# Block attention: the weighing step moved to another place of the round, with 32 named output columns and two buffers of weights

## What is computed

```python
q, k, v = heads(h @ Wq.T), heads(h @ Wk.T), heads(h @ Wv.T)
scores = einsum('bhsd,bhjkd->bhsjk', q, kb) * SCALE
scores = where(diag_mask, -inf, scores)
w = softmax(scores, axis=-1)
w = w * include
out = einsum('bhsjk,bhjkd->bhsd', w, vb)
norm = sum(w, axis=(-2, -1))
o = out / (norm + 1e-06)
return merged(o) @ Wo.T
```

## Time and profile before

| | us |
|---|---|
| median of three runs | 6166.44 |
| the profiled execution | 6168.93 |
| its span | 6167.2 |
| TensorE busy (matmul) | 5278.3 (86%) |
| VectorE busy | 3368.0 (55%) |
| ACT busy | 2937.9 (48%) |
| GpSimd busy | 1177.3 (19%) |

### The profile page before, as it was taken

One profiled execution on the slowest core, in us unless ns is written; L12 is line 12 of the kernel. 1 busy time (PEld: TensorE's weight loads), 2 busy tenths in 40 slices (PEclk: granted clock), 3 DMA queues, 4 the chain that ended last, 5 costly groups with the idle time before them and its releaser, 6 DMA issues. The chain is left out here.

```text
span 6167.2 us, 90780 instructions
## 1 busy us (share of the span) xinstructions
PE 5278.3 (86%) x31918; PEld 3935.3 (64%) x31918; DVE 3368.0 (55%) x6363; ACT 2937.9 (48%) x8715; POOL 1177.3 (19%) x1352
## 2 busy tenths in 40 slices
PE   4799998999989999899997899798879596399968
PEld 2677877877778877778776556455545354255545
DVE  3576676666667666676665333355551654443231
ACT  1566666666666666666664111144441243315421
POOL 1222222222222222223222000111100321002210
PEclk6899999999999999999998999799999798588879
DMA  1000000000000000000001000100000100000000
GB/s 39 15 18 18 16 18 17 18 18 16 15 17 22 18 14 16 18 18 22 13 16 47 1 1 1 70 1 1 0 17 10 23 1 10 28 1 1 1 21 14
DMA packets 49430, 97.37 MB, mean 16 GB/s; under 512 B 12704, under 2 KB 20032, under 8 KB 47840
## 3 DMA queue, kind: packets, MB, share of 16 engines
q1 hardware_dynamic: 48992, 91.77, 5.1%
HBM read 87.28 MB, written 2.38 MB: 15 GB/s over the span
## 5 line engine op out<-in xcount | busy, mean ns | idle before, releaser
L857 ACT ACTIVATE dh_pb<-bank 64x128 f32<-64x128 f32 x3072 | 829.1, 270 | 273.5 <-PE bank L631 239.9
L645 PE MATMUL bank<-dh_cw,dh_pb 128*128 128x128 f32 x5120 | 701.6, 281 | 112.6 <-ACT dh_pb L857 111.1
L645 PEld LDWEIGHTS bank<-dh_cw,dh_pb 128*128 128x128 f32 x5120 | 635.9, 193 | 190.6 <-ACT dh_pb L857 163.9
L995 DVE SCALAR_TENSOR_TENSOR dh_kq<-bank,dh_conv_kq,dh_kq 128x511 f32<-128x511 f32 (+2 forms) x408 | 305.5, 749 | 185.1 <-ACT dh_kq L814 173.9
L863 ACT ACTIVATE dh_cw<-bank 128x256 f32<-128x256 f32 x640 | 244.5, 384 | 255.4 <-PE bank L645 248.1
L582 PE MATMUL bank<-hT,dh_w_kq 128*128 128x512 f32 x544 | 277.7, 635 | 82.7 <-DVE dh_kq L995 75.4
L995 DVE SCALAR_TENSOR_TENSOR dh_v<-bank,dh_conv_v,dh_v 128x511 f32<-128x511 f32 (+2 forms) x384 | 284.2, 747 | 91.2 <-ACT dh_v L814 82.2
L1669 PE MATMUL bank<-moe_h_split,moe_w 128*128 x1200 | 279.7, 383 | 22.2 <-PEq L88 14.9
L594 PE MATMUL bank<-dh_w_vz,hT 128*128 128x256 f32 x1024 | 245.5, 383 | 22.0 <-ACT dh_zs L825 22.0
L582 PE MATMUL bank<-hT,dh_w_vz 128*128 128x512 f32 x512 | 242.5, 596 | 8.5 <-DVE dh_v L995 8.5
L1508 ACT ACTIVATE moe_mlp_silu<-bank 128x512 f32<-128x512 f32 x100 | 59.7, 597 | 394.3 <-PE bank L1675 394.3
(11 more groups left out here) (412 smaller groups left out, 12263.1 us busy)
## 6 DMA issues: line engine op xcount, KB each, us to landing
dh_rates<-delta_rates SPq DMA_DIRECT2D x130, 256.0 KB, 3.6
dh_w_vz<-in_L_wvz SPq DMA_DIRECT2D x17, 512.0 KB, 3.4
mod_w<-in_L_wmod SPq DMA_DIRECT2D x4, 1536.0 KB, 6.8
dh_w_kq<-in_L_wkq SPq DMA_DIRECT2D x18, 256.0 KB, 2.6
dh_wo<-in_L_wo SPq DMA_DIRECT2D x16, 256.0 KB, 4.2
moe_w<-in_L_w13T SPq DMA_DIRECT2D x1, 3200.0 KB, 16.1
x_res<-in_x SPq DMA_DIRECT2D x1, 2048.0 KB, 8.4
mla_wA<-in_L_wA SPq DMA_DIRECT2D x1, 2048.0 KB, 8.0
```

The source lines that it names most:

```text
L645: last = pe.matmul(square(j)[:, b, :, :], pb[j][:, b, :], src[:, :, b, :], start=True, stop=True)
L857: last = act.activation(out[half, :, o, half], src[halves[o], :, half], ACT.Copy)
L995: dve.scalar_tensor_tensor(y, pj_bank(n)[:, 0:S - i], taps(n)[:, TAPS - 1 - i:TAPS - i], y, ALU.mult, ALU.add).then_inc(s["v_cs" if i < TA ...
```

## The change

It moves `weigh` and `shape` on TensorE and VectorE, gives `weights` two buffers, lets `weigh` name 32 output columns for each head (its own 16 features and the 16 that follow in `values`, so the rows of bank 7 between heads hold the next head's result), pads `values` by one head of zeros, puts `oT` into `k.hT`, which is free by then, and makes `tmp` one buffer.

```diff
-        wt = ph.sb("weights", [P, HPG, NC * (NC + 1) // 2 * P])
+        wt = ph.sb("weights", [P, 2 * HPG, NC * (NC + 1) // 2 * P])
...
-        oT = ph.sb("oT", [P, 2, HPG, S])
-        tmp = ph.sb("tmp", [P, 2, 2, D])
+        oT = k.hT
+        tmp = ph.sb("tmp", [P, 2, D])
...
-                            last = pe.matmul(bank[7][32 * i:32 * i + DK2, j * P:S], values[:, b, j, g * HPG + i, :],
-                                             wt[:, i, TURNED_AT[j]:TURNED_AT[j] + (NC - j) * P], start=(j == 0),
+                            head = (b * NC + j) * H2 + g * HPG + i
+                            two = values[:, head:head + 2, :].rearrange("p h n -> p (h n)")
+                            last = pe.matmul(bank[7][32 * i:32 * (i + 1), j * P:S], two,
+                                             wt[:, G % 2 * HPG + i, TURNED_AT[j]:TURNED_AT[j] + (NC - j) * P], start=(j == 0),
                                              stop=(j == NC - 1), skip_group_check=True)
...
-                pe.wait_ge(zero, 1)
+                pe.wait_ge(zero, 2)
...
                     if first: first_pass(G - 1, 0)
-                    if doing["weigh"](G): weigh(G - LAG - 1)
                     if second: second_pass(G - LAG, 0)
...
                     if first: first_pass(G - 1, 2 * RING)
                     if second: second_pass(G - LAG, 2 * RING)
+                    if doing["weigh"](G): weigh(G - LAG - 1)
                     if first: first_pass(G - 1, 3 * RING)
                     if second: second_pass(G - LAG, 3 * RING)
...
-                        after(dve, added, n - 1)
-                        dve.tensor_tensor(tmp[:, i, :, :], ring(("out", b, i))[:, :].rearrange("p (t d) -> p t d", t=2),
+                        after(dve, added, n)
+                        dve.tensor_tensor(tmp[:, :, :], ring(("out", b, i))[:, :].rearrange("p (t d) -> p t d", t=2),
...
                 dve.memset(mx[:, :, :, :], 0.0).then_inc(zero, 1)
-                dve.wait_ge(zero, 1)
+                dve.memset(values[:, NB * NC * H2:, :], 0.0).then_inc(zero, 1)
+                dve.wait_ge(zero, 2)
...
                     if doing["score"](G): maximum(G, 0)
-                    if doing["weigh"](G): shape(G - LAG - 1)
                     if doing["score"](G): maximum(G, 1)
                     if doing["score"](G): maximum(G, 2)
+                    if doing["weigh"](G): shape(G - LAG - 1)
...
-                    after(act, summed if first else weighed, G)
-                    act.activation((e if first else wt)[:, i, at:at + width], ring((which, G, n))[:, 0:width], ACT.Exp)\
+                    after(act, summed if first else weighed, G if first else G - 1)
+                    out = e[:, i] if first else wt[:, G % 2 * HPG + i]
+                    act.activation(out[:, at:at + width], ring((which, G, n))[:, 0:width], ACT.Exp)\
...
-        values = ph.sb("values", [P, NB, NC, H2, DK2])
+        values = ph.sb("values", [P, NB * NC * H2 + 1, DK2])
```

More of the change, by code:

```diff
@@ L2664, in _ @@
                         act.wait_ge(vproj, 2 * b + i + 1)
-                        act.activation(values[:, b, 2 * i:2 * i + 2, :, :].rearrange("p t h n -> p (t h n)"), bank[i][:, :],
-                                       ACT.Copy).then_inc(vkept, 1)
+                        act.activation(values[:, (b * NC + 2 * i) * H2:(b * NC + 2 * i + 2) * H2, :].rearrange("p h n -> p (h n)"),
+                                       bank[i][:, :], ACT.Copy).then_inc(vkept, 1)
         ph.clear()
@@ L2867, in add_out @@
                         xs = k.x[:, b, 2 * i:2 * i + 2, :]
-                        dve.tensor_tensor(xs, xs, tmp[:, i, :, :], ALU.add).then_inc(added, 1)
+                        dve.tensor_tensor(xs, xs, tmp[:, :, :], ALU.add).then_inc(added, 1)
                 dve.memset(mx[:, :, :, :], 0.0).then_inc(zero, 1)
-                dve.wait_ge(zero, 1)
+                dve.memset(values[:, NB * NC * H2:, :], 0.0).then_inc(zero, 1)
+                dve.wait_ge(zero, 2)
                 for G in rounds:
@@ L2914, in clear_corners @@
                         pool.wait_ge(upto, nth(G, HPG * n + i))
-                        ev = t[:, i, at:at + (1024 if n == 1 else 2 * P)].rearrange("p (a n) -> p a n", a=2)[:, :, 0:P]
+                        ev = t(G)[:, i, at:at + (1024 if n == 1 else 2 * P)].rearrange("p (a n) -> p a n", a=2)[:, :, 0:P]
                         pool.affine_select(ev, ev, [[0, 2], [1, P]], ALU.is_ge, 0.0, channel_multiplier=-1).then_inc(done, 1)
                 for G in rounds:
[L2919 to L2922, removed]
+                    if doing["first"](G): clear_corners(lambda G: e, masked1, expd1, G - 1, 0, 1)
+                    if doing["second"](G): clear_corners(lambda G: wt[:, G % 2 * HPG:G % 2 * HPG + HPG], masked2, expd2, G - LAG, 0, 1)
+                    if doing["first"](G): clear_corners(lambda G: e, masked1, expd1, G - 1, 896, 2)
+                    if doing["second"](G): clear_corners(lambda G: wt[:, G % 2 * HPG:G % 2 * HPG + HPG], masked2, expd2, G - LAG, 896, 2)
         ph.clear()
```

## The result

The changed kernel takes **6181.03 us** (median of 20 runs, 6175.69 to 6195.77), the kernel before 6166.07 us in the same session (20 runs, 6159.76 to 6173.71): a ratio of 1.0024, interval 1.0017 to 1.0030. It is slower by 15 us, where 6148 us, 18 us less than before, were forecast. The profiled execution took 6180.93 us (span 6179.2); that of before took 6168.93 (span 6167.2).

The account below looks back on a forecast made before the run. TensorE, busy 86% of the span, was taken as the bound. Steady part -11.5 us, table load +1.8 and tail -8.4 gave -18.1 from the median of 6166.44: 6148 us, range 6140 to 6158.

Parts of the forecast that it names:

- the place: Steady round at full clock: moving the weighing late costs 0.67 us a round, +6.0 us over nine rounds.
- table load: Rounds 10 and 14: the early weighing also hid ACT's table load of 0.90 us; moving it costs +1.8 us.
- the tail: Rounds 16 to 22: gains and losses by round sum to -8.4 us, ends -13 and -4.
- clock term: Steady part: half clock costs 2.95 us a round, of which a third, 1.0 us, stays; -17.5 us.
- the stretch of 71%: Third triples of both passes in round 12: TensorE busy only 71%, right before the clock fell.
- the 87% of F1, S1 and C: Second triples of both passes and the scores after them, round 12: TensorE busy 87%, not followed by a fall.
- rival 3: The weighing runs at half clock, 4.45 us for 2.28: 6176 or 6190 us; decides from 3.0 us a round; chance 0.10.
- Rival 2: Steady part: the clock falls as often as now, each round costs 0.67 us more: 6166 us; chance 0.23.
- F0 to S0: First second-pass triple to first third-pass triple: 1.90 us once the weighing leaves, -1.45 us a round.
- S0 to F1: First third-pass triple to second second-pass triple, scores between: +0.41 us a round, waiting for banks.
- S2 to W: Third third-pass triple to the weighing now behind it: 1.3 us, where 1.87 led to the next triple, -0.57.
- F3 with S3: Fourth triples of both passes: 2.3 us at full clock, between a floor of 2.0 and a ceiling of 3.51.

Follow-up runs that it names:

- run 9: Kernel before, with extra matmuls behind the second and third second-pass triples and the third third-pass triple, none behind the fourth second-pass triple: 6143.53 us, ratio 0.9960.
- run 4: Changed kernel with four extra matmuls of 384 columns behind each of the first three second-pass triples in rounds 7 to 15: 6152.19 us, ratio 0.9979.
- run 7: Changed kernel with the extra matmuls of run 4 behind the second and third second-pass triples only: 6153.52 us, ratio 0.9983.
- run 8: Changed kernel with the extra matmuls of run 4 behind the first second-pass triple only: 6179.12 us, ratio 1.0021.
- run 3: Changed kernel with the weighing split in three parts, one behind each of the first three second-pass triples: 6166.88 us, ratio 0.9996.
- run 1: Changed kernel with the weighing and its shaping back at the old place, columns and buffers kept: 6167.77 us, ratio 1.0000.
- run 2: Changed kernel naming 16 output columns again, the weighing still late: 6180.65 us, ratio 1.0022.
- run 6: Run 3 with extra matmuls of 128 columns behind the third third-pass triple and 256 behind the fourth second-pass triple: 6141.47 us, ratio 0.9962.
- run 10: Run 6 with extra matmuls of 256 columns behind the third third-pass triple and both fourth triples: 6133.87 us, ratio 0.9950.
- run 11: Run 10 with its extra matmuls in rounds 16 to 21 too: 6124.60 us, ratio 0.9935.
- run 5: Kernel before, with extra matmuls behind the second, third and fourth second-pass triples and the third third-pass triple, rounds 7 to 15: 6149.45 us, ratio 0.9974.

## Why the prediction was wrong

The 17.7 us of the steady part split up. At full clock the nine rounds of the old order would take 5 x 21.05 + 2 x 21.60 + 2 x 28.09 = 204.6 us (run 9: plain rounds; round 10, taken for 14 too; round 15 with its projection, taken for 11 too), those of the new order 5 x 22.35 + 2 x 23.40 + 2 x 29.34 = 217.2 (run 4: plain rounds, rounds 10 and 14, round 11). The difference, 12.6 us, is the place: 1.3 us a round, 11.6 in nine, and 1.0 for the logarithm's table load in rounds 10 and 14 (1.05 us each now, 0.55 before). What the traces add to these sums is the clock: 232.3 less 204.6 is 27.7 us before, 250.0 less 217.2 is 32.8 now, 5.1 more. The rows of the result give the same two numbers by another way: 12.6 us more idle time, 5.1 us more busy time. The forecast had +6.0 (place), +1.8 (table load) and -17.5 (clock) in their place, and -8.4 for the tail, which measured -2.0. Of the 33 us between forecast and result, the clock term is about 23.

- **The clock term failed.** It said that a third of the loss stays, 1.0 us a round. The half clock cost 27.7 / 9 = 3.1 us a round before (put at 2.95; the 23.81 had the projection taken off at 9.1 us, of which 2.1 are half clock) and costs 32.8 / 9 = 3.6 now. The forecast took the stretch of 71% alone to be what lets the clock fall and the 87% of F1, S1 and C to be harmless, and it counted on W to lift the clock. But the thin stretch stands before W, so W protects nothing in it. W no longer stands ahead of that stretch, between F0 and S0, and the clock falls in S1, F2 or at W's start. Runs 7 and 8 agree with that, with the reserve made there. W then runs at half clock (4.05 and 3.58 us shown above): rival 3, whose deciding point of 3.0 us a round was passed; its prices, 6176 with half of the loss back and 6190 with none, lie on both sides of the measured 6181, but it had the place at 0.67 as well. Rival 2 (the clock as now) and the Trainium skill's page "TensorE: Matmul & The Clock Gate", section "A second HAM failure mode: psum-queue depth-cycling", were nearer than the forecast. The traces agree with the page in that the clock swings here with no gap above 0.8 us in most rounds, and in run 4 it nearly stops falling once the three gaps are filled. They go beyond it in runs 3 and 9, where it falls with 0.35 us of idle time on record in a round and with none. What else lets it fall stays open.
- **The place was undersized**, 0.67 for 1.3. F0 to S0 is 1.90, as predicted. S0 to F1 was 2.60 and was charged 0.41 more; it takes 3.47 (5733.14 to 5736.61), 0.87 more. The timeline shows where: before, S0 is one run of six records; now the last of them (`x1` at 5734.56) comes 1.42 us after the first, among B's scores, since each of the three tiles waits for a bank of its own. That the score matmuls on the same rows of the array queue behind that tile is read from this order; no run tests it. S0's start as a whole was taken where the start of its last tile counts. S2 to W is 1.45 for 1.3, F3 to T 2.49 for 2.46. So -1.45 + 0.87 - 0.42 + 2.28 + 0.03 = 1.31 us.
- **The tail**, -8.4 forecast and -2.0 measured. Up to round 18's S0 the sum was nearly right (-2.7 forecast, -3.4 measured). Round 18 was to give 3.0 and gives 0.0, round 19 gives -1.2 for 1.7, round 20 gives 0.8 for 3, and round 21 costs 1.1 for 2. Two causes stand in this timeline of TensorE, rounds 17 to 20:

```profile
5867.56 2.36 PE L2793 MATMUL bank<-blk_att_weights,blk_values 128*32 128x512 f32 x32
...
5875.61 2.08 PE L2760 MATMUL bank<-blk_queries,blk_keys 32*128 32x512 f32 x6 [5.05 <-DVE blk_queries L2853]
...
5883.68 4.50 PE L2793 MATMUL bank<-blk_att_weights,blk_values 128*32 128x512 f32 x32
...
5889.59 1.48 PE L2760 MATMUL bank<-blk_queries,blk_keys 32*128 32x512 f32 x6 [0.66 <-DVE blk_queries L2853]
...
5910.40 1.13 PE L2760 MATMUL bank<-blk_queries,blk_keys 32*128 32x512 f32 x6 [2.11 <-DVE blk_queries L2853]
```

The 5.05 us in front of round 18's S0 are the chain of logarithm and subtraction that the forecast named; without W there is nothing to hide it. Behind this pause the clock is low, 0.54 over round 18 (5875.6 to 5889.6), and everything there is longer: S0 to W takes 8.07 us, where it takes 5.28 in round 17 at full clock, and W 4.42, which is 2.1 more than at full clock where 1 was allowed. And the subtraction itself is late in rounds 19 and 20, by VectorE's order:

```profile
5888.24 0.69 DVE L2859 TENSOR_TENSOR hT<-bank,blk_share 128x512 f32<-128x512 f32 x1 [12.69 <-PE bank L2793]
5888.85 0.68 DVE L2853 TENSOR_TENSOR blk_queries<-blk_queries,blk_att_sums 128x512 f32<-128x512 f32 x1
...
5909.06 0.69 DVE L2870 TENSOR_TENSOR x_res<-x_res,blk_att_tmp 128x512 f32<-128x512 f32 x1
5909.66 0.68 DVE L2853 TENSOR_TENSOR blk_queries<-blk_queries,blk_att_sums 128x512 f32<-128x512 f32 x1
```

The shaping, which now waits for the late W, and the additions of the projection stand in front of the subtraction on which S0 waits (0.66 and 2.11 us). The prediction had checked this for the steady rounds alone, where a whole T, A and U lie between, and charged nothing; in the tail nothing lies between. An order with the subtraction ahead of the shaping wasn't tried.
- **The table load was oversized**, 1.8 for 1.0. S0 does start 1.0 us later in rounds 10 and 14 (2.94 after F0 for 1.90, put at 0.90), but the sum took it that W had hidden the load whole; in run 9 the old round carries 0.55 us of it at full clock.
- **Right**: F0 to S0; W behind S2 without a wait for GpSimd; F3 with S3 near the floor (2.3 for 2.46); the columns and buffers at nothing (runs 1 and 2); ACT not the bound.

## What to carry to other kernels

Where the granted clock is under 1 in a stage, first price each round with and without the fall; here about 3 us of each round were the clock, more than any gap in the order was worth. A dense step that is moved behind a thin stretch can itself meet the half clock, as W did here; ask where the clock falls before you count on that step to lift it. Spreading the step over the gaps was worth nothing by itself (run 3) and paid only with extra work beside it (runs 6, 10 and 11). When a step is moved away from between two others, follow the start of the last instruction of each, not the first, on every engine's queue, and follow the rounds at the end apart, since they lack the work that covers an edit in the others. Idle gaps of a pipeline that can't be closed may be worth filling with matmuls whose result is thrown away; measure it, since behind F3 they cost time (run 5).

## What was not expected of the hardware

- Extra work that fits into a gap cost nothing that shows and gave back 29 us on the changed kernel (run 4), 21 on the old order (run 9) and 40 on the old order together with W in parts (run 11): granted clock 0.85 to 0.97, 0.86 to 0.96 and 0.86 to 0.99 in the steady part.
- A TensorE that is recorded as busy for 98% of the stretch (run 3) was granted 0.86 of full clock, one busy for all of it (run 9) 0.96, and one busy 97% (run 4) 0.97. So the recorded busy share does not tell the clock. What in run 3's F3 and S3 lets it fall is left open: the extra matmuls of run 4 are of W's own form, but there are more matmuls in it (1901 records for 1685), and W stands whole behind S2; no run here separates these. Run 3's parts of W and all the extra matmuls use 128 rows of the array, the tiles of both passes 32; whether that counts was not tried.
- The clock falls in the same order of instructions in some rounds and not in others (rounds 10 and 14, which have the longest gap of all, 1.81 us, hold; 7 to 9 don't; in run 2, with 16 columns named, 12 and 13 hold as well); rounds 0 to 6, in the same order in all kernels, took between 116.2 and 125.6 us.
- Named output columns, 16 or 32, changed neither the time of the kernel (6180.65 and 6181.03 us) nor, beyond 0.01, the clock (run 2).
